# A transformer block on one core: the ramp's hand-written orders are re-arranged on five engines

## The reference

```
x = x + xattn(layernorm(x), ctx)        # 16 heads of 64
x = x + ffn(layernorm(x))
ffn(x): h = layernorm(x)*gamma + beta
        h = qlinear(h, w1, b1); h = gelu(h); out = qlinear(h, w2, b2)
qlinear(x, w, b): sx = 127/max|row of x|;  xq = round(x*sx)
        sw = 1/mean|w|;  wq = clip(round(w*sw), -1, 1)
        return xq @ wq.T / (sx*sw) + b
```

## Time and profile before

| | us |
|---|---|
| median of 3 runs | 540.47 (538.56 to 542.25) |
| the profiled execution | 540.51 |
| span of its trace | 538.7 |
| PE busy | 527.3 (98%) |
| DVE busy | 453.6 (84%) |
| ACT busy | 435.9 (81%) |
| POOL busy | 407.3 (76%) |

### The profile page before, as it was taken

One profiled execution on the slowest core, in us unless ns is written; L12 is line 12 of the kernel. 1 busy time (PEld: TensorE's weight loads), 2 busy tenths in 40 slices (PEclk: granted clock), 3 DMA queues, 4 the chain that ended last, 5 costly groups with the idle time before them and its releaser, 6 DMA issues.

```text
span 538.7 us, 8129 instructions
## 1 busy us (share of the span) xinstructions
PE 527.3 (98%) x2434; PEld 227.4 (42%) x2434; DVE 453.6 (84%) x758; ACT 435.9 (81%) x444; POOL 407.3 (76%) x533
## 2 busy tenths in 40 slices
PE   9979989999999999999999999999999999999997
PEld 5433434444444444444444444444444444444443
DVE  3877999999989899988888887988888889887653
ACT  3558899888887888888888888888888889887762
POOL 2288687999998888888888988888888888873300
PEclk9987999999999999999999999999999999999999
DMA  8999233886565656555665556665455574535433
GB/s 310 402 387 294 69 69 102 170 208 162 135 122 141 131 148 119 129 125 130 131 143 142 123 129 117 141 132 132 124 123 130 129 142 103 92 86 100 95 78 98
DMA packets 137015, 78.72 MB, mean 146 GB/s; under 512 B 114246, under 2 KB 114310, under 8 KB 136972
## 3 DMA queue, kind: packets, MB, share of 16 engines
q1 hardware_dynamic: 135636, 75.80, 57.3%
q10 hardware_dynamic: 1335, 2.41, 1.3%
HBM read 33.88 MB, written 17.05 MB: 95 GB/s over the span
## 4 chain that ended last, share of the span: by engine, by line
PE 95%; DVE 3%; POOL 1%; ACT 1%; issue 1%; POOLq 0%; DVEq 0%; ACTq 0%
PE py L1055 41%; PE p L1040 28%; PE pab L1040 14%; PE p L983 3%; PE p L1030 3%; PE pab L1008 2%; PE pab L1030 1%; POOL xr L387 1%; PE pab L968 1%; DVE hx L792 1%; PE py L1016 1%; PE py L1008 1%; DVE w2q L779 1%; ACT hid L578 0%; PE py L974 0%
## 5 line engine op out<-in xcount | busy, mean ns | idle before, releaser
L1055 PE MATMUL py<-w2q,hqT 128*128 128x512 bf16 x1024 | 231.0, 379 | 1.7 <-DVE hqT L829 1.7
L587 ACT ACTIVATE hq<-hid,hscale 128x2048 int8<-128x2048 f32 x64 | 128.1, 2002 | 46.2 <-DVE hscale L821 46.2
L1040 PE MATMUL p<-w1q,xqT 128*128 128x512 bf16 x688 | 159.4, 380 | 0.0
L1055 PEld LDWEIGHTS py<-w2q,hqT 128*128 128x128 bf16 x1024 | 100.1, 98 | 123.0 <-DVE hqT L829 2.7
L578 ACT ACTIVATE hid<-p,xdeq 128x1024 f32<-128x1024 f32 x86 | 95.0, 1106 | 15.9 <-PE p L1040 11.2
L1040 PEld LDWEIGHTS p<-w1q,xqT 128*128 128x128 bf16 x688 | 63.8, 98 | 81.2 <-issue 10.1
L387 POOL TENSOR_TENSOR xr<-xr,attn 128x512 f32<-128x512 f32 x64 | 83.3, 1320 | 18.7 <-DVE attn L727 17.2
L402 POOL TENSOR_TENSOR hx<-hx,beta_b 128x512 f32<-128x512 f32 x64 | 91.7, 1454 | 4.4 <-ACT hx L563 4.3
L815 DVE TENSOR_REDUCE hmax<-hid 128x1 f32<-128x1025 f32 x64 | 78.1, 1220 | 18.0 <-ACT hid L578 17.4
L406 POOL TENSOR_TENSOR xr<-xr,b_b 128x512 f32<-128x512 f32 x64 | 92.6, 1465 | 0.0
L809 DVE TENSOR_REDUCE hid<-hid 128x1 f32<-128x1024 f32 x64 | 77.4, 1209 | 8.8 <-ACT hid L578 8.8
(11 more groups left out here) (88 smaller groups left out, 408.9 us busy)
## 6 DMA issues: line engine op xcount, KB each, us to landing
xr<-x SPq DMA_DIRECT2D x64, 256.0 KB, 2.9
out<-xr SPq DMA_DIRECT2D x64, 256.0 KB, 2.4
raw<-w1T SPq DMA_DIRECT2D x8, 512.0 KB, 12.2
hid<-wvT SPq DMA_DIRECT2D x8, 256.0 KB, 7.8
wout<-wout_d ACTq DMA_DIRECT2D x8, 256.0 KB, 8.7
wout<-w2T SPq DMA_DIRECT2D x3, 512.0 KB, 5.5
xr<-w2T SPq DMA_DIRECT2D x2, 512.0 KB, 11.1
attn<-ctxm_d SPq DMA_DIRECT2D x4, 256.0 KB, 8.1
```

What stands on the lines that cost most here:

```text
L587: nc.scalar.activation(hq8[:, t % 2, :], hid[:, t % 2, 0:HID], ACT.Copy, scale=col(hscale, t))\
L1040: mm = nc.tensor.matmul(hidden_bank(t, n), xT[:, k, :], w1q[:, k, n * D:(n + 1) * D], start=False, stop=(k == KD - 1))
L1055: mm = nc.tensor.matmul(py[:, t % 2, :], hqT[:, t % 2, c // 2, c % 2, :], w2q[:, c, :], start=(c == 0), stop=(c == 2 * NJ - 1))
```

## The change

Five lists are re-ordered; no instruction is added, removed or given another shape, and the loops from tile 6 on are unchanged. One wait is split: `out_rows` waited for all four copies of Wv Wout, and now its k-th matmul waits for the first k + 1.

On PE, `out_rows(2)` (the rows of batch 3) goes from ahead of `first_layer(0)` to behind it, so that two of them, `out_rows(0)` and `out_rows(1)`, come ahead of it; `weight_total(1)` and `tail_product` go between `first_layer(1)` and `bias(2)`, `out_rows(3)` behind `first_layer(2)`. On SP, the context's loads go ahead of w2's, and the transposes of x tiles 0 to 3 go ahead of some loads. On DVE, ACT and POOL the calls of the ramp are interleaved anew.

```diff
@@ SP
             load_x(4)
+            load_ctx()
             load_w2(0)
             load_b1_rows()
             load_x(5)
             load_w2(1)
-            load_ctx()
             load_w2(2)
+            transpose_x(0)
             load_x(6)
             load_w2(3)
             load_w2(4)
-            transpose_x(0)
+            transpose_x(1)
             load_w2(5)
...
             load_x(9)
+            transpose_x(2)
+            transpose_x(3)
...
@@ POOL
             add_attention(1, 1)
-            add_attention(2, 1)
-            add_attention(3, 1)
             pool.wait_ge(const_set, 3)
             inverse_std(0, 1)
+            add_attention(2, 1)
             inverse_std(1, 1)
             pool.wait_ge(beta_loaded, 16)
             add_beta(0, 1)
+            add_attention(3, 1)
+            add_beta(1, 1)
             inverse_std(2, 2)
-            add_attention(4, 1)
-            add_beta(1, 1)
-            add_attention(5, 1)
             widen_x(0, 1)
...
@@ ACT
             times_std(0)
             abs_w1(5)
-            copy_wvo(2)
             times_std(1)
             abs_w1(6)
+            copy_wvo(2)
+            round_x(0)
             abs_w1(7)
-            round_x(0)
             times_std(2)
             times_std(3)
+            round_x(1)
             abs_w2(0)
             copy_wvo(3)
             round_weights(0, 1)
             round_weights(0, 3)
             abs_w2(1)
-            times_std(4)
-            times_std(5)
-            round_x(1)
             abs_w2(2)
-            abs_w2(4)
             abs_w2(3)
-            abs_w2(5)
-            abs_w2(6)
-            abs_w2(7)
             gelu(0, 0)
             round_x(2)
             gelu(0, 1)
             round_x(3)
+            abs_w2(4)
+            abs_w2(5)
+            abs_w2(6)
+            abs_w2(7)
+            gelu(1, 0)
+            times_std(4)
+            gelu(1, 1)
+            times_std(5)
             round_weights(1, 0)
             round_weights(1, 1)
+            round_h(0)
+            round_weights(1, 2)
+            gelu(2, 0)
+            round_weights(1, 3)
+            gelu(2, 1)
+            round_h(1)
+            round_weights(1, 4)
             round_x(4)
             round_x(5)
...
             round_weights(1, 5)
+            widen_h(0)
             round_weights(1, 6)
-            widen_h(0)
             round_weights(1, 7)
-            times_std(7)
             gelu(3, 0)
             gelu(3, 1)
+            times_std(6)
+            times_std(7)
             round_h(2)
@@ DVE
             statistics(1)
+            centre(1)
+            abs_w1(4)
             statistics(2)
+            centre(2)
             statistics(3)
-            abs_w1(4)
-            centre(1)
-            centre(2)
+            centre(3)
             x_scale(0, 1)
-            centre(3)
-            statistics(4)
             weight_sum(0)
-            centre(4)
+            x_scale(1, 1)
             weight_scale(0)
-            statistics(5)
-            x_scale(1, 1)
+            round_w1(0)
+            clip(0, 0)
+            clip(0, 1)
+            round_w1(2)
+            clip(0, 2)
+            clip(0, 3)
+            x_scale(2, 2)
             ctx_sum(0)
             ctx_sum(1)
             ctx_sum(2)
...
             attn_rows(1)
+            ctx_means()
+            statistics(4)
+            half_scale(0)
+            centre(4)
+            hidden_scale(0)
+            statistics(5)
             attn_rows(2)
+            centre(5)
+            half_scale(1)
             weight_sum(1)
-            ctx_means()
+            hidden_scale(1)
             weight_scale(1)
...
@@ PE
             def out_rows(i):
                 b = (i + 1) % B
-                pe.wait_ge(wvo_copied, KD)
...
                 for k in range(KD):
+                    pe.wait_ge(wvo_copied, k + 1)
...
             out_rows(0)
             out_rows(1)
             bias(0)
-            out_rows(2)
             first_layer(0, 0)
             first_layer(0, 1)
-            weight_total(1)
+            out_rows(2)
             bias(1)
             first_layer(1, 0)
             first_layer(1, 1)
-            out_rows(3)
+            weight_total(1)
+            tail_product()
             bias(2)
             first_layer(2, 0)
             first_layer(2, 1)
-            tail_product()
+            out_rows(3)
             bias(3)
```

65 lines of the change are left out of this document (21 added, 44 removed).

## The result

| | before | changed |
|---|---|---|
| median, us | 540.42 (538.56 to 543.05, 12 runs) | 545.29 (542.60 to 548.49, 12 runs) |
| ratio | 1 | 1.0091 [1.0069, 1.0113] |
| span of the trace | 538.7 | 543.1 |

The change makes the kernel 0.9% slower, 4.9 us. The forecast was 539.5 us, 1 us faster.

What follows compares the result with a forecast made beforehand. PE was taken to bound the kernel, so only the start of `second_layer(3)` could move. Terms 1 to 5, chained, brought it about 1.0 us earlier: 540.5 - 1.0 = 539.5 us, range 535.3 to 543.2.

Steps and rivals of the forecast that it cites:

- What bounds the kernel: PE, 98% busy, bounds it; only the start of `second_layer(3)` can move, with 11.3 us recoverable including the low clock.
- Term 1: PE's gap ahead of `weight_total(0)`: w1's sum reaches PE at 36.5 against 37.66, 1.2 us earlier, bounds 0 and 3.5.
- Term 2: PE's first stretch: clock falls about where it did, ends a little sooner; `first_layer(0)` at 49.3, PE 4 us ahead by `first_layer(1)`.
- Term 3: w2's sum on DVE: PE gets it at 62.5, a new 2.2 us wait; w2's scale at 64.2, 4.4 us later.
- Term 4: ACT's list after w2's scale takes 22.5 us, so `second_layer(1)` can start at 86.7, 1.4 us earlier; PE waits about 0.8.
- Term 5: DVE up to `second_layer(3)`: `x_scale(6)` starts at 85.3 instead of 86.21, so `second_layer(3)` comes 0.9 to 1.0 us earlier.
- A price that could differ: POOL's additions beside DVE's two w1 roundings: each could lose up to 1.3 us, a loss of up to 1.6 us overall.
- DVE isn't late: Rival, chance 0.13: w2's scale comes where it came before, and the kernel takes 531.5 us.
- The clock stays high: Rival, chance 0.27: PE's first gap is too short for the clock to fall, and the kernel takes 537.6 us.
- The clock falls twice: Rival, chance 0.15, slower: the wait for w2's sum is a second PE gap of 2.2 us and more.

Runs made afterwards that it cites:

- x1: Changed kernel with ACT taking the last eighth of the w1 sum ahead of rounding tile 0: 543.57 us, 1.0097 of the kernel before.
- x3: Changed kernel with w2's sum and scale two and five calls earlier on DVE: 547.15 us, 1.0164 of the kernel before.
- x2: Changed kernel with both gelus of tile 1 ahead of the deviation multiplication of tile 4 on ACT: 543.91 us, 1.0099 of the kernel before.
- q1: Changed kernel with POOL adding b2 to tiles 2 and 3 behind the widening of tiles 6 and 7: 546.91 us, 1.0106 of the kernel before.
- c3: c2 with POOL adding b2 to tiles 0 to 2 ahead of widening tiles 2 and 3: 537.53 us, 0.9964 of the kernel before.
- z2: Changed kernel, w1's last eighth ahead of rounding tile 0, both DVE roundings ahead of clips, tile 1's gelus and tile 9's row earlier: 541.98 us, 1.0024.
- c2: Kernel before with a shorter way to w1's scale and DVE's two w1 roundings moved into its waits for tiles 4 and 5: 539.91 us, 0.9984.

## Why the prediction was wrong

**What bounds the kernel.** Right as to the place: nothing behind `second_layer(3)` moved. Wrong as to the engine. PE's waits and its clock are "what there is to win" only as far as DVE does not hold it back. x1 took 2.3 us and the low clock away from PE's first stretch, x3 its second gap, and neither is measurably faster than the changed kernel.

**Term 1 (the gap ahead of `weight_total(0)`) failed: 37.72, not 36.5.** My chain left out `inverse_std(1, 1)`, 1.1 us on POOL ahead of tile 0's beta; tile 3's row was done at 32.3 instead of 31.3. `centre(2)` then held DVE until 32.77, 1.74 us long beside POOL. The scale of tile 0 was ready at 35.5 instead of 34.4, and the rest followed as forecast. This was the bound that I had given, a gain of 0. The scale of w1 came at 38.65 (forecast 37.65).

**Term 2 held in its sum, the clock by luck.** In this trace the clock fell at 37.9, 0.2 us after PE had started again behind its gap of 3.04, and came back at 41.3, 5.6 us sooner than before and not "a little"; that made good the 1.2 us of term 1. In the second trace of the same kernel a gap of 3.02 us stood there and the clock stayed at 2.4 GHz. Windows of the changed kernel, first trace, beside the earlier trace rows:

```profile
38.00:40.00 2.00, 2.00 (x4) 0.97 (x5) 1.86 (x6) 1.94 (x3) 1.11 (x2) 0.50 0.33 129
40.00:42.00 2.00, 2.00 (x5) 0.85 (x4) 0.85 (x2) 0.72 (x3) 1.78 (x5) 0.68 0.00 0
```

`first_layer(0)` started at 48.72 (49.3). PE was 3.2 us ahead at `first_layer(1)` (forecast 4; `out_rows(2)` waited 1.32 for DVE). The two parts that the text gives for `first_layer(0)`, 2.2 and 3.6, add up to 5.8, while 55.62 less 49.3 is 6.3; nothing further is built on them.

**Term 3: the sum right, the scale not.** From w1's scale to w2's sum I had 24.65 us and the trace has 24.95, and PE's new wait is 2.66 (2.2). But the scale comes 3.1 us behind the sum instead of 1.9. Timeline of ACT:

```profile
63.18 0.72 ACT L563 ACTIVATE hx<-hx,rstd 128x512 f32<-128x512 f32 x1 [2.44 <-POOL rstd L394]
63.81 1.10 ACT L578 ACTIVATE hid<-p,xdeq 128x1024 f32<-128x1024 f32 x1
...
66.90 1.15 ACT L553 ACTIVATE w2q<-xr,wscale 128x1024 int16<-128x1024 f32 x1 [1.38 <-DVE wscale L765]
...
88.49 1.06 ACT L596 ACTIVATE hqT<-hT 128x1024 bf16<-128x1024 int8 x1
```

`times_std(4)` stands ahead of `gelu(1, 1)`, needs a deviation that POOL makes only behind `statistics(5)`, near the end of DVE's list, and `hidden_scale(1)` waits for that gelu. x2 takes exactly this away, and x3 makes the scale 6 us earlier, and neither is faster: the step was wrong, and it alone was not the cause of the loss.

**Term 4: ACT's length right, PE's waits not.** From 66.90 to the end of the second widening at 89.55 are 22.65 us; forecast 22.5. PE waited 2.33 + 1.68 at `second_layer(0)`, not 0.8, since DVE came late with the widening and with the clips that stood beside POOL.

**Term 5 is the step that failed.** I worked out `x_scale(6)` along ACT and POOL (85.3) and took for granted that DVE would be free. In the trace it starts at 90.56: DVE works from 74.58 on without a pause and is the last to come. The 5.3 us are made up, along my own path, of 2.7 because ACT gets w2's scale later (terms 1 and 3), 0.2 in ACT's list, 1.05 because POOL's beta for tiles 6 and 7 ends 2.55 us behind ACT and not 1.5 (89.3), and 1.3 for which DVE is still busy. So in this trace ACT and POOL alone would have made the call 3.1 us later than before too; that it is DVE's list that binds is shown by x3, where they are ready at 87.0 and DVE comes at 91.2.

What should have been summed is DVE's own list between two fixed instructions: its length in the trace before, less the waits that the new order removes, plus those that it makes. Two of the latter could be read from the orders, the sum behind `round_x(0)` (1.9) and `clip(0, 1)` behind ACT's rounding (3.3, in the forecast 3.2); terms 1 and 3 have them on the way to the sums, term 5 has nothing of DVE. The two by themselves would not have given a loss: they are 5.2 us, and the listed waits of before 6.9. It takes the rest as well, the wait for gelu (1.2), the waits for POOL's rows that stay (2.0) and the 2.2 us of longer instructions, and of those the forecast had none.

**A price that could differ** was no aside. The place was wrong: w1's roundings lost 0.1 us in all (1.31 + 2.29 against 3.5 before; 2.6 in the second trace), and w2's clips, which the text didn't name, lost 1.6 in both traces. The Trainium skill, "SBUF — State Buffer", section "Who interferes with whom", says that of two instructions on the shared ports the one issued second blocks until the first ends. By that rule, as an estimate, a clip loses up to one of POOL's additions. The traces agree: a clip of 128x1024 takes 0.35 us with POOL idle (q1, c3), 0.74 in the changed kernel and 1.28 in x3, the length of one of POOL's additions there (1.26).

**The rivals.** "DVE isn't late" was the opposite of what happened (and DVE's idle time between 30 and 60 us of the trace before is 4.6 us, not 6). "The clock stays high" did occur, in the first gap of the second trace, and that execution took 544.32 us and not 537.6. "The clock falls twice" occurred too, the second time at the tail's product (5.36 us for 8 matmuls, 3.60 before), but that is not what sets the end: x1, in whose trace the clock didn't fall at all ahead of `second_layer(0)`, isn't measurably faster than the changed kernel. No run shows a length of gap that decides the fall; what they show stands below. No rival had DVE's list as the bound, and the range ended 2.1 us below the measured time.

**What stays open.** z2 has before's stretch and is still 0.24% [0.05, 0.43] slower. Its longer instructions are within that stretch and can't be what is left over; its first copy stood 2.05 us later than in the trace before, and whether that is chance one trace doesn't tell. How much of the loss is idle time and how much longer instructions is read from single traces (1.5 and 1.3 us in the second). The intervals of c2 and c3 overlap, so the gain of that step is read from their traces and from c3's verdict against before. No run has SP's new list alone; in the trace of the changed kernel no engine waits for a transfer between 22.8 and 90.6 us except ACT, 0.23 us for an eighth of w2.

## What to carry to other kernels

Before moving work in a hand-written pipeline, find the engine whose list leads without slack to the last fixed point, and sum that list, busy and idle apart, between two instructions that both versions have; a wait of another engine that is removed pays only if it shortens that list. A call moved up on the waiting engine is paid where its producer stands: check every wait ahead of it in the producer's list. Work of POOL can cost DVE time where both run, so put it where DVE waits anyway and nobody waits for POOL; DVE's small instructions beside it are then what it costs (c3).
